# Four graph layers on one core: the first layer's second half written out tile by tile

## What is computed

```
u   = mish([x, agg] @ W3 + b3)          # first half
y   = x + u @ W4 + b4                   # second half
x   = layernorm(x + layernorm(y) * gamma + beta)
```

## Time and profile before

| | |
|---|---|
| median of 3 runs | 1433.16 us |
| lowest, highest | 1428.68, 1433.31 us |
| profiled execution, its own time | 1435.59 us |
| its span, first to last instruction | 1433.9 us |
| mean granted TensorE clock | 0.947 of full |
| busy: PE, DVE, ACT, POOL | 88%, 72%, 60%, 47% of the span |

### The profile page before, as it was taken

One profiled execution on the slowest core, in us unless ns is written; L12 is line 12 of the kernel. 1 busy time (PEld: TensorE's weight loads), 2 busy tenths in 40 slices (PEclk: granted clock), 3 DMA queues, 4 the chain that ended last, 5 costly groups with the idle time before them and its releaser, 6 DMA issues. The chain is left out here.

```text
span 1433.9 us, 19078 instructions
## 1 busy us (share of the span) xinstructions
PE 1265.1 (88%) x5927; PEld 1016.0 (71%) x5927; DVE 1026.9 (72%) x1798; ACT 853.3 (60%) x762; POOL 677.8 (47%) x473
## 2 busy tenths in 40 slices
PE   2955999999999999999999971797778994998998
PEld 2844778888788888788888851586566883886886
DVE  3222899999999999999999991345853337847345
ACT  1115999999999999999999970345322101321211
POOL 0027778888888888888888511002610001011000
PEclk9986999999999999999999995798989997999999
DMA  5668767777777777777777512876003310000001
GB/s 188 256 228 186 155 142 142 160 153 155 154 154 158 161 158 155 150 151 152 154 152 147 93 20 37 307 259 219 30 30 110 134 31 29 13 4 1 1 8 66
DMA packets 103430, 179.34 MB, mean 125 GB/s; under 512 B 34818, under 2 KB 40112, under 8 KB 103368
## 3 DMA queue, kind: packets, MB, share of 16 engines
q0 software_dynamic: 70032, 104.09, 37.1%
q1 hardware_dynamic: 30848, 69.56, 14.1%
q10 hardware_dynamic: 2488, 4.89, 1.0%
HBM read 138.59 MB, written 37.11 MB: 123 GB/s over the span
## 5 line engine op out<-in xcount | busy, mean ns | idle before, releaser
L476 POOL DMA_INDIRECT G<-q_dram,idx_all x168 | 346.3, 2061 | 54.6 <-issue 45.9
L755 PE MATMUL ps_x<-w_hi,hT_hi 128*128 128x512 f32 x672 | 269.0, 400 | 1.3 <-DVE hT_lo L554 1.3
L755 PE MATMUL ps_x<-w_lo,hT_hi 128*128 128x512 f32 x672 | 262.4, 390 | 0.0
L755 PE MATMUL ps_x<-w_hi,hT_lo 128*128 128x512 f32 x672 | 261.6, 389 | 0.0
L468 POOL DMA_INDIRECT G<-p_dram,idx_all x168 | 173.5, 1033 | 146.6 <-issue 143.4
L755 PEld LDWEIGHTS ps_x<-w_hi,hT_hi 128*128 128x128 f32 x672 | 126.2, 188 | 31.5 <-issue 1.7
L755 PEld LDWEIGHTS ps_x<-w_hi,hT_lo 128*128 128x128 f32 x672 | 126.2, 188 | 27.4
L755 PEld LDWEIGHTS ps_x<-w_lo,hT_hi 128*128 128x128 f32 x672 | 126.2, 188 | 25.2
L717 PE MATMUL ps_x<-ident,G 128*128 128x128 f32 x672 | 103.5, 277 | 30.6 <-DMA G<-q_dram,idx_all 23.0
L561 DVE TENSOR_TENSOR x<-ps_x,b 128x512 f32<-128x512 f32 x168 | 114.9, 684 | 20.1 <-PE ps_x L755 18.1
L717 PEld LDWEIGHTS ps_x<-ident,G 128*128 128x128 f32 x672 | 85.9, 144 | 54.5 <-DMA G<-q_dram,idx_all 23.4
(11 more groups left out here) (252 smaller groups left out, 2859.4 us busy)
## 6 DMA issues: line engine op xcount, KB each, us to landing
ea_raw<-in_eaT SPq DMA_DIRECT2D x84, 128.0 KB, 4.4
adj_dram<-adj_sb POOLq DMA_DIRECT2D x42, 210.2 KB, 4.6
adj_dram<-zeros SPq DMA_DIRECT2D x11, 640.5 KB, 4.2
adj_in<-adj_dram SPq DMA_DIRECT2D x10, 640.0 KB, 4.7
adjT_dram<-adjT_sb SPq DMA_DIRECT2D x10, 640.0 KB, 5.9
adjT_rest<-adjT_dram SPq DMA_DIRECT2D x8, 640.0 KB, 8.9
w_raw_n<-in_w SPq DMA_DIRECT2D x4, 1024.0 KB, 7.8
agg_dram<-agg_sb POOLq DMA_DIRECT2D x42, 84.0 KB, 9.4
```

Of the source, the lines that this page charges most:

```text
L476: g.indirect_dma_start(G[:, b.slot, c * D:(c + 1) * D], None, q_dram, bass.IndirectOffsetOnAxis(ap=idx_all[:, i:i + 1], axis=0), compute_o ...
L755: last = t.matmul(ps_x2[c % 2][:, :], h[:, b.slot, e], w[:, k, :], start=(k == 0 and i == 0), stop=(k == KD - 1 and i == 2))
```

## The change

In words, all in `first_layer`:

- **The neighbours' product has two banks.** `ps_n` is a list of two; PE's wait for `xlo_ready` is now for the tile before the previous one. To make room, the y products use `ps_T[1][0]` and `ps_out`.
- **X is turned in place.** The copies by SP (`x_new_load`, `xn`) are gone; PE's transposes read `X` and wait for `x_new`. Turn and product of tile n now stand in the same step, three behind its y product.
- **Sines.** `SIN_FIRST = 6`: ACT takes the Sine of tiles 0 to 5 inside the first half, after its work of step 8, and of tiles 6 to 9 after its last Arctan.
- **The u products start earlier.** PE turns `us` of tile 0 between the two products of the last tile of the first half. W4 goes to the first half of the weight tiles and W_l to the second (hence `slot_w`), and both are split in four slices of 512 columns: W4 by ACT and DVE in the last step, W_l over steps 0 to 2.
- **The per-tile order of DVE and ACT is new** and there are no loops in the second half. `mv`, `sd`, `rs` and `nmr` have two slots. In a step DVE now does the whole outer layernorm of tile s-1 up to `nmr` before it takes up y of tile s.
- Degrees are computed in four parts in steps 0 to 3. Gamma and beta are loaded after `d_ready`, into storage of `adj_in`, no longer behind the landing of the last adjacency stores.

Core of the diff (semaphore lists and unchanged pieces are left out):

```diff
+        ps_y, ps_nT = [ps_T[1][0], ps_out], [ps_T[1][1], ps_adj3[:, 0:D]]
+        ps_n = [ps_adj3[:, D:2 * D], ps_adj3[:, 2 * D:3 * D]]
...
-                def x_new_load(s):
...
-                    sp.wait_ge(x_new, s.count(1))
-                    sp.dma_start(xn[s.slot], X[:, cols(s.number())]).then_inc(row_in[s.slot], 16)
```

ACT, in the first half and then in the second:

```diff
+                    if s.it2 is None and s.k == R:
+                        act.wait_ge(w4_in, 16)
+                        act.wait_ge(w3a_used, 1)
+                        for k in range(KD):
+                            a.copy(w_hi[:, k, :], w_raw[:, k, :]).then_inc(w4_hi, 1)
+                        turned_high(0)
...
+                    if s.it2 is None and s.k == R - 2:
+                        sine(0, SIN_FIRST)
                 tile_steps(act, -1, R, step)
+                turned_high(1)
+                sine(SIN_FIRST, R)
+                act.wait_ge(w_next_in[0], 16)
+                act.wait_ge(z_out, R)
+                for s in range(0, R + 4):
+                    if s >= 4:
+                        act.wait_ge(z_out, R + s - 3)
...
+                        a.copy(U_hi[:, cols(s - 4)], ps_n[s % 2]).then_inc(z_ready, 1)
+                    if 3 <= s < R + 3:
+                        act.wait_ge(T_ready, 2 * R + s - 2)
+                        a.copy(T_hi[1][:, (s - 3) % 2, :], ps_nT[(s - 3) % 2][:, :]).then_inc(hi_ready, 1)
+                    if 1 <= s < R - 1:
+                        turned_high(s + 1)
+                    c = s - 1
+                    if 0 <= c < R:
+                        act.wait_ge(mv_ready[1], c + 1)
+                        a.activation(sd[1][:, c % 2:c % 2 + 1], mv[1][:, c % 2, 1:2], ACT.Sqrt, bias=eps_col[:, :]).then_inc(sd_ready[1], 1)
+                        act.wait_ge(co_ready, c + 1)
...
+                        a.activation(X[:, cols(c)], y_out[:, c % 2, :], ACT.Identity, scale=rs[1][:, c % 2:c % 2 + 1],
+                                     bias=nmr[:, c % 2:c % 2 + 1]).then_inc(x_new, 1)
+                    for k in ((0, 1), (2,), (3,))[s] if s < 3 else ():
+                        a.copy(w_hi[:, KD + k, :], w_raw[:, KD + k, :]).then_inc(wn_hi, 1)
+                    if s < R:
+                        act.wait_ge(mv_ready[0], s + 1)
+                        a.activation(sd[0][:, s % 2:s % 2 + 1], mv[0][:, s % 2, 1:2], ACT.Sqrt, bias=eps_col[:, :]).then_inc(sd_ready[0], 1)
```

POOL (`u_of`, `with_b4` and `with_beta` are the three operations of before, with their waits):

```diff
+                u_of(0)
+                u_of(1)
                 wait(aT_ready, R)
                 wait(d_ready, R)
+                with_b4(0)
+                for s in range(R):
+                    if s + 1 < R:
+                        with_b4(s + 1)
+                    if s == 0:
                         wait(gb_in, 32)
+                        wait(aT_out[1], 16 * (R // 2))
+                    with_beta(s)
+                    if s + 2 < R:
+                        u_of(s + 2)
```

DVE, one step (the low parts of the turned u, `turned_low`, and of the weights as before):

```diff
+                    if 0 <= c < R:
+                        dve_.wait_ge(sd_ready[0], c + 1)
+                        v.reciprocal(rs[0][:, i:i + 1], sd[0][:, i:i + 1]).then_inc(rs_ready[0], 1)
...
+                    if 0 <= e < R:
+                        dve_.wait_ge(hi_ready, 2 * R + e + 1)
...
+                    if 1 <= s < R - 1:
+                        turned_low(s + 1)
...
+                    if 0 <= f < R:
+                        dve_.wait_ge(z_ready, R + f + 1)
+                        v.tensor_tensor(U_lo[:, cols(f)], ps_n[f % 2], U_hi[:, cols(f)].bitcast(F32), ALU.subtract).then_inc(xlo_ready, 1)
...
+                        dve_.wait_ge(sd_ready[1], c + 1)
+                        v.reciprocal(rs[1][:, i:i + 1], sd[1][:, i:i + 1]).then_inc(rs_ready[1], 1)
...
+                    if s < R:
+                        dve_.wait_ge(y_ready, s + 1)
+                        dve_.wait_ge(xb_ready, s + 1)
```

PE (`turn_u` is the turn of `us` of before):

```diff
+                            if i == 0 and s.it2 is None and s.k == R - 1:
+                                last.then_inc(w3a_used, 1)
+                                turn_u(0)
...
+                for s in range(0, R + 3):
+                    n = s - 3
+                    if n >= 0:
+                        pe.wait_ge(x_new, n + 1)
...
+                            last = t.transpose(ps_nT[n % 2][:, k * P:(k + 1) * P], X[:, n * D + k * P:n * D + (k + 1) * P], ident[:, :])
+                        last.then_inc(T_ready, 1)
+                    if s + 1 < R:
+                        turn_u(s + 1)
+                    if s < R:
+                        pe.wait_ge(u_lo, s + 1)
...
+                        three_products(nc, ps_y[s % 2], T_hi[0][:, s % 2, :], T_lo[0][:, s % 2, :], w_hi[:, 0:KD, :], w_lo[:, 0:KD, :],
                                        True, True).then_inc(y_ready, 1)
...
+                    if n >= 0:
...
+                        if n >= 2:
+                            pe.wait_ge(xlo_ready, n - 1)
+                        pe.wait_ge(lo_ready, 2 * R + n + 1)
+                        three_products(nc, ps_n[n % 2], T_hi[1][:, n % 2, :], T_lo[1][:, n % 2, :], w_hi[:, KD:, :], w_lo[:, KD:, :],
                                        True, True).then_inc(z_out, 1)
```

More of the change, by code:

```diff
@@ L38 @@
 EXACT = 4096
-SIN_TILES = (2, 6)
+SIN_FIRST = 6
 EPS = 1e-5
@@ L888, in _ @@
                 tile_steps(sp, -2, R - 1, step)
-                for u in range(2):
-                    sp.wait_ge(aT_out[u], 16 * (R // 2))
+                sp.wait_ge(d_ready, R)
                 for t, b in ((gam, g0), (bet, be0)):
@@ L893, in _ @@
                 for u in range(2):
+                    sp.wait_ge(aT_out[u], 16 * (R // 2))
+                for u in range(2):
                     sp.dma_start(adjT[:, u, :], adjT_dram[u * P:(u + 1) * P, :]).then_inc(adj_first[u], 16)
-                def x_new_load(s):
-                    if s.at(-2).real():
-                        sp.wait_ge(T_ready, s.at(-2).count(1) + 2 * R)
-                        sp.sem_inc(turn, 1)
-                    sp.wait_ge(x_new, s.count(1))
-                    sp.dma_start(xn[s.slot], X[:, cols(s.number())]).then_inc(row_in[s.slot], 16)
-                tile_steps(sp, 0, R - 1, x_new_load)
             @block.scalar
@@ L910, in _, with sine, turned_high @@
                     act.dma_start(t[:, :], bcast(b)).then_inc(c_in, 16)
+                def sine(r0, r1):
+                    c = slice(r0 * D, r1 * D)
+                    act.wait_ge(atan, r1)
+                    a.activation(TH[:, c], TH[:, c], ACT.Sin, scale=-2.0, bias=half_pi[:, :]).then_inc(t_ready, 1)
+                def turned_high(r):
+                    if r >= 2:
+                        act.wait_ge(y_ready, r - 1)
+                    act.wait_ge(u_T, r + 1)
+                    a.copy(T_hi[0][:, r % 2, :], ps_T[0][r % 2][:, :]).then_inc(u_hi, 1)
                 def step(s):
@@ L986, in _, with u_of, with_b4 @@
                 wait(T_ready, 2 * R)
+                def u_of(r):
+                    if r >= 2:
+                        wait(u_T, r - 1)
+                    if r in (0, SIN_FIRST):
+                        wait(t_ready, 1 if r == 0 else 2)
+                    g.tensor_tensor(us[:, r % 2, :], Z[:, cols(r)], TH[:, cols(r)], ALU.mult).then_inc(us_ready, 1)
+                def with_b4(r):
+                    if r >= 2:
+                        wait(y_used, r - 1)
+                    g.tensor_tensor(xb4[:, r % 2, :], X[:, cols(r)], b4[:, :], ALU.add).then_inc(xb_ready, 1)
@@ L1016, in _, with turned_low @@
                 v = nc.vector
+                def turned_low(r):
+                    dve_.wait_ge(u_hi, r + 1)
+                    v.tensor_tensor(T_lo[0][:, r % 2, :], ps_T[0][r % 2][:, :], T_hi[0][:, r % 2, :].bitcast(F32), ALU.subtract).then_inc(u_lo, 1)
                 def step(s):
+                    if s.it2 is None and s.k == R:
+                        for k in range(KD):
+                            dve_.wait_ge(w4_hi, k + 1)
+                            v.tensor_tensor(w_lo[:, k, :], w_raw[:, k, :], w_hi[:, k, :].bitcast(F32), ALU.subtract).then_inc(w4_lo, 1)
+                        turned_low(0)
                     b = s.at(-1)
@@ L1123, in _, with turn_u @@
                 t = nc.tensor
+                def turn_u(r):
+                    pe.wait_ge(us_ready, r + 1)
+                    for k in range(KD):
+                        last = t.transpose(ps_T[0][r % 2][:, k * P:(k + 1) * P], us[:, r % 2, k * P:(k + 1) * P], ident[:, :])
+                    last.then_inc(u_T, 1)
                 def turn_both(b):
```

272 lines of the change are left out of this document (99 added, 173 removed).

## The result

The changed kernel takes **1427.14 us** (median of 20 runs, 1422.56 to 1431.66) against 1432.14 (20 runs of the kernel before on the same chip): ratio **0.9963, 95% interval 0.9952 to 0.9974**. It is 5 us faster, less than the half per cent that the prediction counts as no change, and not the forecast 19.6. The profiled execution took 1428.67 us, its span is 1427.0 (before 1435.59 and 1433.9).

The account below looks back on a forecast made before the run. PE's waits and a low clock were taken to bound the second half of `first_layer`, then DVE with ACT. First root 1000.5, steps 62.0 and the tail gave 1079.4 against 1099.0, hence 1413.5 us, range 1405 to 1424.

Parts of the forecast that it names:

- the half per cent: Whole kernel: a measurement can tell about 0.5%, 7.2 us, from no change.
- Start, forecast 8.0 us: Start of the second half: first root of tile 0 at 1000.5 in place of 1008.45, 8.0 us earlier.
- drain: Rival at ACT's four table loads before the first root: each costs as much again, 5.2 us, time 1419; chance 0.03.
- Steps, forecast 62.0 us from the first to the tenth root: Second half: nine steps bound by DVE with ACT, middle ones 7.15 us, 62.0 in all, tenth root at 1062.5.
- the scaling with x + beta (L1096 before) 0.65: Middle step on DVE: this scaling takes 0.65 us, one term of the 7.2 us sum.
- otherwise lie beside ACT: Inner reciprocal and subtraction (L1082 before): beside ACT in other steps, counted as 0.9 us only in steps 1 and 2.
- the upper bound: Whole kernel, 1422: six handovers a step 0.1 us longer, scaling slowed 0.2 by POOL, 7 us, and 1 to 2 at the start.
- The longer chain, my rival of 8.3 us a step: Second-half steps: DVE and ACT wait longer on ACT's in-order stream, nine steps 1.1 us longer, time 1423.5; chance 0.14.
- Tail, forecast 16.9 us: Tenth root to block end: product 7 at 1064.6, products 8 and 9 at 4.9 us each, end at 1079.4.
- Sum: Block end at 1079.4 against 1099.0, 19.6 us off; median 1413.5.
- The later layers: Layers after the block: the same work, starting cold behind the barrier as before, so 0 us.
- The chance: Whole kernel: 0.94 for faster by more than 7.2 us, a time under 1426; 0.03 the same, 0.03 slower.

Follow-up runs that it names:

- e1: Changed kernel with POOL's three operations of a second-half tile over 8 of 512 columns, output incomplete; 1411.86 us, one run.
- e2: Changed kernel with one POOL wait set later, so x + beta of a tile begins behind y_out of the tile before; 1417.05 us, ratio 0.9893.
- e7: Changed kernel with one operand of y_sc (gamma) replaced by a PSUM bank, output without the gains; 1418.68 us, one run.
- e3: Kernel before with only the second bank for the neighbours' product added; 1413.49 us, ratio 0.9872.
- e6: Changed kernel with one bank for the neighbours' product instead of two; 1433.21 us, ratio 1.0002.
- e10: e2 with the turns of X of tiles 8 and 9 ahead of products 7 and 8, high and low parts likewise; 1413.40 us, ratio 0.9862.
- e5: Kernel before's second-half order on ACT, DVE and POOL, with two banks, X turned in place and the changed kernel's early start; 1409.07 us, ratio 0.9834.
- e8: e5 with POOL's three operations of a step begun only behind y_out of two tiles before; 1410.87 us, ratio 0.9848.

## Where the prediction was right and where it failed

- **Start, forecast 8.0 us: right.** The first root came 7.4 us earlier, 7.9 against the copy of tile 8. No drain stood at a table load: each took 1.28 us, with ACT's neighbouring rows 0.02 us away, once 0.10.
- **Steps, forecast 62.0 us from the first to the tenth root: this failed,** with 70.4. The failed step is an overlap that I put at nothing: POOL beside DVE. It sits in two places of the middle step. One is the term "the scaling with x + beta (L1096 before) 0.65": `y_out` took 1.07 to its successor. The other is the clause that the inner reciprocal and the subtraction "otherwise lie beside ACT" and so cost nothing: the turned X's low part starts 2.09 us behind the inner root (1040.66 to 1042.75), behind `y_sc` with its 1.76, where the sum has 1.4. Together that is 1.1 us. The rest of the sum holds, 4.41 measured for 4.55.
- **How I came to it.** The earlier trace rows had the warning, 5.25 us beside POOL for what took 2.29 without it, and I applied it to the weight slices only; for the scaling I put 0.2 us into the upper bound. The durations of L1082 and L1096 came from an order in which they stood ahead of POOL's operations or clear of them, and I never laid POOL's three operations beside DVE's in the new order. Had I done so, L1136 would have shown as POOL's release, and 3.8 us of POOL as covering both. With POOL out of the way, the working holds: nine steps of 60.1 us in e1 and 63.0 in e2, middle steps of 6.97 and 7.07.
- The rule that I missed: the Trainium skill, page "SBUF — State Buffer", section "Who interferes with whom", says that an instruction of VectorE with two SBUF inputs contends with one of GpSimd (POOL here) that reads SBUF, and that the ports they share are an exclusive lock, so that the one issued second waits for the whole of the other. The trace agrees: e7's `y_out` ended 0.55 us behind POOL's operation, and `y_sc` with one PSUM input was not held up (0.75).
- **The longer chain, my rival of 8.3 us a step,** comes near the 8.17 by luck, with the wrong reason: in the middle steps the root stood behind nothing on ACT, `U_hi` did not wait for PE, and the 0.36 us waits were as in the forecast.
- **Tail, forecast 16.9 us: 19.2.** Product 7 starts 2.1 us behind the tenth root, as forecast. From it to product 8 it is 7.6 us (5.4 forecast), from there to product 9 5.05 (4.9 forecast). Nearly all of the miss of 2.3 is product 7, 5.26 us at the low clock in place of 2.86; I had let the clock be full there.
- **Sum.** -19.6 forecast; +0.6 for the start (the first half ended 0.5 later in this execution), +8.4 for the steps, +2.3 for the tail: -8.3, which is 1090.70 against 1099.01. The later layers add 1.4 (forecast 0), which I take for scatter: -6.9 in the spans, -5.0 in the medians.
- **The largest gap was one that I didn't ask about.** I priced the change as one piece. PE's 17.3 us were to be had with the bank alone (e3), and in the new order the bank hardly counts in the steps (e6, 2.1 us of nine steps). By its parts the change is: bank 20 us, start 2 to 4, and the new order takes about 18 back. Of these some 10 go through POOL (e2) and 4 through its tail (e10). The other 4, by which e10 still stands above e5, hide a larger sum: from the first to the tenth root e10 takes 63.0 us and e5 54.9, while e10's start is 2.6 shorter and its tail 2.3. That those 8.1 us of steps come from the chain of single roots is argued (7.07 us a step against 5.4 to 6.3), not tried by itself.
- **The chance.** "Faster" meant a time under 1426, with 0.94. Every case had one loss at a time; the slower steps and the slower tail together led to 1427.14.

## What to carry to other kernels

When an order is rewritten, take durations from the old one only for operations whose neighbours stay; for each operation of VectorE with both inputs in SBUF, write down which operation of GpSimd runs at that time in the new order and which of the two is issued first, and add the remainder to the second. A wait on GpSimd is cheap to move: one constant gave 10 us here. But it pays only where its product is not needed earlier (e8). And price each part of a change alone: the second bank, one of the smallest edits, carried the gain.

## What the runs showed of the hardware

- A DVE operation on 128x512 (fp32) with both inputs in SBUF took 0.72 to 0.75 us alone and 0.85 to 2.52 when it was issued inside one of POOL's; it then ended 0.54 to 0.56 us behind POOL's (in the changed kernel, e5, e7 and e8). POOL's took 1.25 to 1.31 alone and 1.5 to 2.0 when DVE's was ahead of it. Operations of DVE with one input in PSUM took 0.67 to 0.69 (0.72 to 0.75 for `y_sc` in e7) beside POOL.
- The one that waits is not always served next: in e5 `y_out`, issued at 1005.73, waited out the operation in flight and also the next one of POOL, begun at 1006.41; it ended at 1008.25, 0.56 behind that one. In the changed kernel `y_sc` got in between two of POOL's. What decides it, no run here shows.
- The same wait of PE, 3.05 us for the turned X's low part, was followed by a product of 5.26 us in the changed kernel and of 4.42 in e2, against 2.86 at the full clock.
